# Moving one piece of split-off radial rows and the mixed matrix to other places in VectorE's order

## What is computed

```
xn = layernorm(x)
# edges: radial features (64 per edge) -> gate -> message -> sum per target node
gate = sigmoid(silu(edge_attr_64 @ W1 + b1) @ W2 + b2)
aggr = segment_sum(gate * xn[src], dst)
upd  = silu(concat([xn, aggr]) @ U1 + c1) @ U2 + c2
# linear attention over all nodes, 4 heads of 64
kv   = einsum('bhsd,bhse->bhde', layernorm(xn @ wk.T), layernorm(xn @ wv.T)) / S
mix  = (xn @ wq.T) @ kv @ wo.T + bo
x    = x + (xn + upd) + mix
x    = x + mixture_of_experts(layernorm(x))     # top 2 of 16 experts
```

## Time and profile before

| | |
|---|---|
| median of 3 runs | 1086.65 us (1086.01 to 1088.88) |
| the profiled execution, its own time | 1086.7 us |
| its span, first to last instruction | 1084.7 us |
| busy share of the span: PE / DVE / ACT / POOL | 96% / 82% / 64% / 69% |
| chain that ended last, by engine | PE 86%, DVE 8%, issue 2%, ACT 1%, DMA 1% |

### The profile page before, as it was taken

One profiled execution on the slowest core, in us unless ns is written; L12 is line 12 of the kernel. 1 busy time (PEld: TensorE's weight loads), 2 busy tenths in 40 slices (PEclk: granted clock), 3 DMA queues, 4 the chain that ended last, 5 costly groups with the idle time before them and its releaser, 6 DMA issues.

```text
span 1084.7 us, 23741 instructions
## 1 busy us (share of the span) xinstructions
PE 1042.7 (96%) x7960; PEld 983.1 (91%) x7960; DVE 886.8 (82%) x1495; ACT 696.9 (64%) x1091; POOL 748.9 (69%) x705
## 2 busy tenths in 40 slices
PE   5998999999999999999999998999899999999995
PEld 2556899999999999999999998998699999999995
DVE  7997988888999888889888883488687777777773
ACT  4765667766666666666666644656277777777763
POOL 5475777777777777777777766540357777777765
PEclk9999999999999999999999999999999999999998
DMA  7212445444444544444454420226278989889961
GB/s 254 76 54 70 140 141 147 142 143 139 139 144 142 146 142 142 137 141 145 142 145 143 141 80 22 79 69 192 52 218 223 239 218 235 218 231 222 233 189 15
DMA packets 118528, 159.75 MB, mean 147 GB/s; under 512 B 20568, under 2 KB 91052, under 8 KB 118444
## 3 DMA queue, kind: packets, MB, share of 16 engines
q1 hardware_dynamic: 86780, 91.60, 26.1%
q0 software_dynamic: 31104, 66.28, 26.1%
q10 hardware_dynamic: 560, 0.79, 0.2%
HBM read 142.42 MB, written 18.17 MB: 148 GB/s over the span
## 4 chain that ended last, share of the span: by engine, by line
PE 86%; DVE 8%; issue 2%; ACT 1%; DMA 1%; POOL 0%; DVEq 0%; POOLq 0%; ACTq 0%; PEldq 0%
PE ps L1748 25%; PE ps L1955 16%; PE ps L1759 16%; PE ps L1700 8%; PE ps L1967 8%; PE ps L1801 4%; PE ps L1813 2%; PE ps L1826 2%; PE ps L1675 1%; PE ps L1935 1%; DVE st L1090 1%; PE ps L1840 1%; DVE ssq L1107 1%; PE ps L1881 1%; PE ps L1684 1%
## 5 line engine op out<-in xcount | busy, mean ns | idle before, releaser
L1748 PE MATMUL ps<-fr 128*128 128x256 f32 x2352 | 305.6, 286 | 0.8 <-DVE fr L1152 0.5
L1748 PEld LDWEIGHTS ps<-fr 128*128 128x128 f32 x2352 | 288.2, 191 | 1.7 <-DVE fr L1152 1.6
L644 POOL DMA_INDIRECT big<-xn_rows,srcs x200 | 218.7, 1093 | 61.2 <-issue 61.2
L644 POOL DMA_INDIRECT hgx<-xn_rows,srcs x192 | 210.1, 1094 | 58.5 <-issue 58.5
L826 ACT ACTIVATE h1f<-ps,b 128x512 f32<-128x512 f32 x196 | 124.1, 684 | 170.6 <-PE ps L1700 169.4
L1759 PEld LDWEIGHTS ps<-oh,big 128*128 128x128 f32 x1568 | 191.2, 193 | 8.6 <-DVE big L1299 0.5
L1955 PE MATMUL ps<-fr 128*128 128x256 f32 x1536 | 190.5, 283 | 1.5 <-issue 1.3
L1759 PE MATMUL ps<-oh,big 128*128 128x96 f32 x1568 | 189.7, 274 | 0.4 <-DVE big L1308 0.4
L1955 PEld LDWEIGHTS ps<-fr 128*128 128x128 f32 x1536 | 186.8, 192 | 2.3 <-issue 2.1
L1152 DVE TENSOR_TENSOR fr<-h1f,fr 128x1024 fp32r<-128x1024 f32 x98 | 120.5, 1229 | 48.4 <-ACT fr L829 48.3
L719 POOL DMA_INDIRECT out<-xnT,idx x60 | 113.3, 1889 | 41.6 <-issue 34.7
(11 more groups left out here) (246 smaller groups left out, 1421.1 us busy)
## 6 DMA issues: line engine op xcount, KB each, us to landing
big<-in_w SPq DMA_DIRECT2D x128, 256.0 KB, 4.3
rbf<-in_rbf SPq DMA_DIRECT2D x98, 256.0 KB, 3.0
big<-in_w SPq DMA_DIRECT2D x32, 512.0 KB, 4.4
xn_rows<-xn SPq DMA_DIRECT2D x26, 128.0 KB, 2.4
big<-xn_rows,srcs POOLq DMA_INDIRECT x200, 3.1
xn_rows<-hgx SPq DMA_DIRECT2D x24, 128.0 KB, 2.4
hgx<-xn_rows,srcs POOLq DMA_INDIRECT x192, 3.2
out<-x_nodes SPq DMA_DIRECT2D x6, 512.0 KB
```

Source lines behind the costliest of these rows:

```text
L644: pool.indirect_dma_start(hg[i % HB][:, s, :], None, xn_d[:, :], bass.IndirectOffsetOnAxis(srcs[:, col:col + 1], 0))\
L1748: last = mm(ps[:, 2 + 4 * p + s // 2, (s % 2) * D:(s % 2 + 1) * D], h1s[p][a][:, c, s * P:(s + 1) * P], W2s[b][:, c, :], start=c == 0 and ...
```

## The change

Two edits, both on DVE alone. `rbf_low` for group 2 moves from its place between `mix_a1` and h1_low(1) to the stage of keys and values, ahead of the scaling of the last tile. `mix_m` moves from between step(0) and step(1) into step(1), behind h1_low(3) and ahead of onehot(1).

```diff
@@ stage of keys and values
                     kv_step(last, 2)
                 if u == NT - 4:
                     rbf_low(0, 1, 1)
+                if u == NT - 2:
+                    rbf_low(0, 2, 0)
             h1_low(0, 0, 0)
@@ edges(n0, w0, w_n, base, rel_t, mix=...)
-                def step(i, h, p, before=3, after=3):
+                def step(i, h, p, before=3, after=3, between=nothing):
 
                     bias(i, p)
                     if after > 2:
@@
                     if after > 1:
                         h1_low(n0, i + 2, p)
+                    between()
                     onehot(i, p)
                     message(i, h, p)
@@
                 mix[0]()
                 mix[1]()
-                rbf_low(n0, 2, 0)
+                if mix[0] is nothing:
+                    rbf_low(n0, 2, 0)
                 h1_low(n0, 1, 1)
                 step(0, (0, 0), 0, before=0)
-                mix[2]()
-                step(1, (1, 0), 1, before=1)
+                step(1, (1, 0), 1, before=1, between=mix[2])
                 step(2, (2, 0), 0, before=2)
```

## The result

The changed kernel is slower: 1146.28 us median (1139.10 to 1152.99, 4 runs) against 1086.33 us for the kernel before (1085.94 to 1088.88) beside it, a ratio of 1.0538 with a 95% interval of 1.051 to 1.0565. The prediction was 1084.2 us. The profiled execution took 1152.99 us, with a span of 1151.0.

What follows compares the result with a forecast made beforehand. TensorE was taken as the bound, held up by one wait for rbf_low and the low clock behind it. Terms of -2.48 and +0.10 made -2.4 us, from a median of 1086.65 to 1084.2 us; range 1083.2 to 1086.0.

Steps and rivals of the forecast that it cites:

- What bounds the kernel: Whole chain: mostly TensorE; at the edge stage's start up(4) waits 1.88 us for rbf_low(4), then the clock falls.
- part two: Start of edge stage: mix_m behind h1_low(3) brings up(4) to 112.81 and gains 2.48 us.
- The clock: Rival at up(4): PE's clock falls despite the shorter pauses, giving 1085.2 us; chance 0.20.
- The row against it: Stretch from 88 to 92: granted clock still 1.00 after 1.10 us of PE idleness at 90.80.
- Part one: Keys and values stage: rbf_low(2) ahead of tile 24's scaling gains nothing and costs 0.1 us, bounds 0 and 0.4.
- The step that failed: From up(5) on, PE's earlier start counts fully at the end: 2.48 us gained, no cost for gathers in the sum.
- rivals of 0.08 and 0.04: POOL's gathers fall behind: gain given back at the end, 1085.9 us (0.08), or slower than before, 1087.7 us (0.04).
- The prediction's own sign for it: The whole is wrong if PE shows another wait of over half a microsecond between 122 and 640.
- The slow pace: POOL's gathers beside a busy VectorE: 5.96 us from group 4 to 5, against a mean of 5.59.
- five to ten slow groups: Groups of gathers at 5.96 us: five more make 1085.9 us, ten make 1087.7 us.
- The rival at the end: End of edge stage: the last message waits about 1.7 us for late gathers, giving 1085.9 us; chance 0.08.
- The rule weighed in the prediction: Keys and values stage: POOL's scaling fully holds the moved rbf_low(2) until 93.83; time about 0.2 us higher.

Runs made afterwards that it cites:

- e1: The kernel before with only mix_m moved into step 1, the low rows of group 2 at their old place: 1151.21 us, ratio 1.0567.
- e3: The changed kernel with 3 of the 4 gathers of a group from group 4 on: 1085.00 us, ratio 0.9976.
- e4: The changed kernel with h1_low and message each cut into two instructions of half the size: 1084.21 us, ratio 0.9962.
- e9: The kernel before with only mix_m moved, and h1_low and message each cut into two: 1084.35 us, ratio 0.9974.
- e11: The changed kernel with h1_low and message each cut into two, measured once more: 1083.05 us, ratio 0.9969.
- e7: The kernel before, order unchanged, with POOL's first gather held until VectorE has copied the product with wo: 1165.90 us, ratio 1.0713.
- e2: The kernel before with only the low rows of group 2 moved, mix_m at its old place: 1087.56 us, ratio 1.000.
- e6: The changed kernel with two fills of spare tiles behind the message in steps 2 to 9: 1085.77 us, ratio 0.9985.
- e10: The changed kernel with h1_low and message cut into two and rbf_low(5) also moved into step 1, ahead of mix_m: 1086.93 us, ratio 0.9999.

## Why the prediction was wrong, step by step

- **What bounds the kernel, and part two on PE: right.** Wait gone (0.27 us left, forecast 0.28), no fall of the clock, up(5) held by rbf_low(5) (0.42 to 0.44 us, forecast 0.3 or a little more), scatter(1) at 120.22 in e1 (forecast 120.16). Where the gathers don't get in the way, the gain is about the forecast one: against the kernel before (655.35) the node stage begins 2.76 us earlier in e3 (652.59) and 1.6 to 2.3 us earlier in e4, e9 and e11, where 2.4 was the forecast. By their medians e4, e9 and e11 are 0.26% to 0.38% below the kernel before, 2.8 to 4.1 us, but the cut alone gave 0.14%, 1.5 us.
- **The clock.** From 112 to 122 it is 1.00 in all eight traces with part two, so this rival didn't come. The row against it, though, was weaker than it looked: the 1.10 us pause at 90.80 that left the clock at 1.00 stands at the same place in the traces of the changed kernel and of e7, and there the lower clock followed it.
- **Part one: right, and small.** The moved instruction took 0.99 us beside POOL (forecast 1.09), the scaling of tile 24 came 0.09 later by it (forecast 0.07), and e2 shows no difference in time. That the 1.63 us of h1_low agrees with a full hold by POOL, as the prediction has it, is so only roughly: held until 95.22, h1_low would end at 96.45, and it ended at 96.29. It is the same with the moved instruction in e2: held until POOL's 93.96 it would end at 94.65, and it ended at 94.51.
- **The step that failed** is the one that put the gathers at nothing in the sum: "a microsecond that up(5) comes earlier is a microsecond of the end, as long as nothing else becomes late", with the gathers left to rivals of 0.08 and 0.04. The rival was named in the right place (gathers that fall behind a VectorE without pauses), but its price was 1087.7 us where 1146 was measured. The prediction's own sign for it came: between 122 and 640 `up` waits 29 times for `rbf_low`, 35.5 us in all, up to 2.8.
- **Why the price was wrong.** The slow pace, 5.96 us a group, was read off one group, whose four gathers met one h1_low and one message (1.55 and 1.30 us); group 4 of the changed kernel takes the same 5.96 (119.63 to 125.59). In the steps of 4.98 us that follow, three gathers fit, one of them held by h1_low and one by the message each time, so a group costs 4.99 / 3 x 4 = 6.65 us, and VectorE asks for one every 4.98. By that the lead goes at 1.7 us a step, not 0.4; in the trace it falls from 9.27 us at group 3 to 3.25 at group 7, 1.5 a step. And the sentence "nothing in the profile shows a lasting slow pace" took the 5.59 us of the gathers as a pace of their own. POOL's own is 4 x (0.95 + 0.30) = 5.0 us; the rest is the holds that it meets in VectorE's step, and they were as regular as that step because each gather met the same instruction again. A pace that equals another engine's to the hundredth calls for the question whether it is tied to it, and the prediction treated it as independent.
- **Why it lasts.** The prediction counted five to ten slow groups, and the short steps are indeed few: in e3, where no message waits for a gather, VectorE's pauses are back before h1_low at 144.4, after four steps of 4.98 to 5.09 us. By then the lead of the changed kernel is gone, and the slow pace stays. From group 5 on its gathers need (708.53 - 125.59) / 371 x 4 = 6.29 us a group (371 gathers after the first of group 5), 0.70 above the kernel before, and 93 groups of that are 65 us. e7 shows that this course keeps itself up without the change's order.
- **The rival at the end** (the last message waits for its gather) came where PE was early and the gathers were not early with it: 1.5 us in e6, 1.1 in e10.
- **The rule weighed in the prediction** (the Trainium skill, SBUF — State Buffer, section "SBUF: two separate sides": a VectorE instruction with two inputs in SBUF and a GpSimd instruction that reads SBUF exclude each other) was weighed only for POOL's scaling of the values, where it moved 0.2 us. The gathers read their row numbers from SBUF (`srcs`), and the traces show such a hold there, with 0.82 us from the end of VectorE's instruction to the end of the gather; whether it is this read that is held, no run here shows. Applied to every gather that a denser VectorE would meet, the rule would have given the loss its place.

## What to carry to other kernels

Before an order is tightened, look at what runs beside the stall: here VectorE's pauses were what let four of POOL's gathers into a step, and closing a 1.9 us wait on TensorE cost 60 us. Where two engines show the same period, ask which one sets it and whether the other has a pace of its own; count how many of its instructions fit into one period when the pauses are gone, and how long the lead lasts. Long two-input instructions on VectorE can be cut in halves at 0.06 us each, which bounds what a gather can be held for.

## What the runs showed of the hardware

In these traces an indirect gather of 128 rows takes 0.94 to 0.95 us on POOL when it starts with VectorE idle (90 gathers of the changed kernel), or with more than 0.3 us left of a bias, which reads PSUM and one tile in SBUF (14 gathers there; the one at 263.11 ran wholly within a bias). When it starts with more than 0.3 us left of an h1_low or a message, which read two tiles in SBUF, it ends 0.81 to 0.83 us after that instruction; so did all 92 gathers of the changed kernel that met an h1_low, and 76 of the 78 that met a message. The other two started within 0.03 us of the message's own start (261.86 and 462.58); they took the plain 0.95, and the message took 1.25 and 1.28 us instead of 1.22. So the hold goes almost wholly one way: a gather can lose more than 1 us (it took up to 1.99 us in the changed kernel), and VectorE's instruction lost at most 0.08 to a gather (an rbf_low of 0.77 instead of 0.69, in e1), and only where the two start together. Beside POOL's scaling of values VectorE loses more: in e2 a 0.69 us instruction took 0.99. And a one-off lag of some 8 us, more than the lead that the gathers have over their landing (8.8 - 3.1 = 5.7 us), can put a kernel into a course in which a group takes 6.35 us instead of 5.59 to the end of the stage, with every run in it (1160.78 to 1173.17 in e7).
